# The second alignment's code differences moved from TensorE's fp32 products to VectorE's bf16 operations

## What is computed

```python
D = _pairwise_euclidean(small, large)          # 1601 x 64 per batch
R = _dtw_cost(D)                               # R[i,j] = D[i,j] + min(R[i-1,j], R[i,j-1], R[i-1,j-1])
i_idx, j_idx, valid = _backtrack(R, T_small, T_large)   # choice = argmin([diagonal, up, left])
expanded = zeros.at[j_idx].add(small[i_idx] * valid)
x = x + align(ctx_1024, layernorm(x))          # 32 batches; small = ctx_1024 (1601 rows), large = x (64 rows)
x = x + rwkv(layernorm(x))                     # 4 x 512 tokens, 256 features, 16 heads
x = x + moe(layernorm(x))                      # 8 experts of 704, the best 2 of each token, and a shared one
```

## Time and profile before

| | |
|---|---|
| median of 3 runs | 1171.64 us (1171.23 to 1174.55) |
| span of the profiled execution | 1175.4 us |
| mean granted TensorE clock | 0.938 |
| TensorE busy | 1005.5 us, 86% |
| VectorE busy | 660.5 us, 56% |
| ScalarE busy | 494.2 us, 42% |
| lines 1590 and 1591, both alignments | 68.5 and 63.5 us busy, 144 records each |
| chain that ended last, by engine | TensorE 55%, VectorE 29%, DMA 6%, ScalarE 3% |

### The profile page before, as it was taken

One profiled execution on the slowest core, in us unless ns is written; L12 is line 12 of the kernel. 1 busy time (PEld: TensorE's weight loads), 2 busy tenths in 40 slices (PEclk: granted clock), 3 DMA queues, 4 the chain that ended last, 5 costly groups with the idle time before them and its releaser, 6 DMA issues.

```text
span 1175.4 us, 15523 instructions
## 1 busy us (share of the span) xinstructions
PE 1005.5 (86%) x4892; PEld 598.2 (51%) x4892; DVE 660.5 (56%) x2311; ACT 494.2 (42%) x847; POOL 115.5 (10%) x150
## 2 busy tenths in 40 slices
PE   5886639888891799997899699887999999999998
PEld 2332213333330455553576465645676767676776
DVE  4994949999999776487669612427311111111116
ACT  4885627766781345423242155243222222222221
POOL 1000000000000000000000000000252425242210
PEclk9998979999996799988899799799999999999999
DMA  9999954565876989440050097394121212123115
GB/s 354 324 309 272 274 155 141 154 190 157 237 225 163 327 252 329 135 150 11 1 186 1 0 336 249 104 349 174 49 83 57 83 56 84 56 84 105 32 52 182
DMA packets 123806, 190.47 MB, mean 162 GB/s; under 512 B 9008, under 2 KB 93136, under 8 KB 123728
## 3 DMA queue, kind: packets, MB, share of 16 engines
q1 hardware_dynamic: 117840, 171.13, 47.0%
q0 software_dynamic: 5888, 18.36, 5.1%
HBM read 165.43 MB, written 24.03 MB: 161 GB/s over the span
## 4 chain that ended last, share of the span: by engine, by line
PE 55%; DVE 29%; DMA 6%; issue 4%; ACT 3%; SPq 2%; POOL 0%; DVEq 0%; ACTq 0%; POOLq 0%
PE bank L1816 13%; PE bank L1663 8%; PE bank L1847 7%; PE bank L1684 4%; DVE table L825 4%; PE bank L1808 3%; DMA spaced<-dist 3%; DVE beyond L841 3%; DVE passed L846 3%; PE bank L1827 3%; DVE col_min L818 2%; DVE z L756 2%; PE bank L1590 2%; PE bank L1839 2%; PE bank L1811 2%
## 5 line engine op out<-in xcount | busy, mean ns | idle before, releaser
L1028 DVE TENSOR_TENSOR hid<-bank,act_s 128x352 f32<-128x352 f32 x104 | 54.2, 524 | 220.9 <-PE bank L1816 182.1
L1816 PE MATMUL bank<-w_up,srcT 128*128 x512 | 162.9, 460 | 0.8 <-ACT srcT L1434 0.8
L1574 PE MATMUL bank<-sq,ones 128*64 128x402 f32 (+1 forms) x512 | 101.3, 517 | 38.2 <-ACT sq L1291 38.2
L1442 ACT ACTIVATE act_s<-bank 128x352 f32<-128x352 f32 x104 | 47.9, 463 | 198.4 <-PE bank L1816 127.7
L1816 PEld LDWEIGHTS bank<-w_up,srcT 128*128 128x128 f32 x512 | 96.0, 189 | 47.9 <-issue 4.1
L1590 PE MATMUL bank<-table,ident 128*128 128x402 f32 x144 | 68.5, 560 | 56.3 <-DVE stays L789 51.0
L1568 PE MATMUL bank<-ctxT,latT 128*64 128x402 f32 (+1 forms) x512 | 101.2, 517 | 4.8 <-DMA ctxT<-ctx_tr_dram 4.0
L1663 PE MATMUL bank<-rows_c,on_path 128*64 128x256 f32 (+1 forms) x832 | 100.8, 395 | 2.4 <-DMA rows_c<-ctx_nat_dram 1.6
L1291 ACT ACTIVATE sq<-ctxT 128x1608 f32<-128x1608 f32 x64 | 97.5, 1526 | 8.5 <-DMA ctxT<-ctx_tr_dram 8.5
L1847 PE MATMUL bank<-w_dn,hidT 128*128 (+1 forms) x384 | 93.6, 380 | 0.4 <-DVE y_sb L1042 0.4
L1328 ACT ACTIVATE code<-bank,unpassed 128x402 bf16<-128x402 f32 x72 | 42.1, 589 | 122.9 <-PE bank L1592 122.9
(11 more groups left out here) (292 smaller groups left out, 1619.5 us busy)
## 6 DMA issues: line engine op xcount, KB each, us to landing
rows_c<-ctx_nat_dram SPq DMA_DIRECT2D x32, 896.0 KB
ctxT<-ctx_tr_dram SPq DMA_DIRECT2D x32, 804.0 KB, 8.7
ctxT<-ctx_tr_dram SPq DMA_DIRECT2D x32, 797.0 KB, 7.5
rows_c<-ctx_nat_dram SPq DMA_DIRECT2D x32, 640.0 KB
spaced<-dist SPq DMA_DIRECT2D x128, 101.0 KB, 3.8
w_up<-w_t_dram SPq DMA_DIRECT2D x16, 704.0 KB, 13.3
table<-spaced SPq DMA_DIRECT2D x48, 202.0 KB, 4.2
w_dn<-w_t_dram SPq DMA_DIRECT2D x16, 256.0 KB, 5.8
```

Of the source, the lines that this page charges most:

```text
L1028: e.tensor_tensor(hid[i][:, :], psum[2 * i + 1][:, 0:HH], act_s[i][:, :], ALU.mult).then_inc(hid_done, 1)
L1574: last = e.matmul(ps[b * T:(b + 1) * T, 0:nq], ones[:, 0:T], sq[i][:, b, k, 0:nq], start=False, stop=(k == KC - 1))
L1816: last = e.matmul(psum[2 * i + m][:, 0:HH], srcT[t % 2][:, k, :], w_up[:, bass.ds(ex, 1), m, k, columns], start=(k == 0), stop=(k == KC - 1))
```

## The change

For the second alignment (g = 1) only, TensorE's `code_gap` and ScalarE's `code_bar` are dropped. In their place, for a block q:

- VectorE, step 4q+4, behind `code_stays`: `code_lead`, table row minus `col_min` for the whole block (804 columns), rounded to bf16 in `lead`.
- ScalarE, n = 4q+5: `code_faint`, `stays` times TIE/2 into the one buffer `faint`.
- VectorE, step 4q+6, between the minimum and the scan: `code_lean`, `lead` minus `faint` in bf16. It waits for `code_faint`.
- ScalarE, n = 4q+7: `code_shut`, Relu of `lead` times -PASSED/FAINT into the code, and the edge column.
- VectorE, step 4q+9: `code_final`, now in the second block after instead of the third. It waits for `code_shut`.

The last block is closed on VectorE alone by three dependent operations (`code_last`), and ScalarE only writes its edge. `col_min` and `stays` have two buffers instead of three in the second group, and the memset of the third at its start goes. The first alignment (g = 0) keeps its products, and its waits are the same.

```diff
-MINIMA = [2, 3]
+PLACES = 2
+FAINT = TIE / 2
+def late_faints(n):
+    return [n // CB - 1] if n >= CB and n % CB == 1 else []
+def late_shuts(n):
+    return [n // CB - 1] if n >= CB and n % CB == 3 else []
-        col_min.append(place("col_min2", [CB, L]))
-        stays.append(place("stays2", [CB, LW], BF16))
+        lead, faint = [place(f"lead{i}", [CB, L], BF16) for i in range(2)], place("faint", [CB, L], BF16)
 # VectorE
+            def code_lead(q):
+                tb, k0, n, i = table[1], q * CB, code_width(q), q % 2
+                if q >= 2:
+                    e.wait_ge(shut, q - 1)
+                e.tensor_tensor(lead[i][:, 0:n, :], tb[:, k0 + 1:k0 + n + 1, 0:L], col_min[i][:, 0:n, :],
+                                ALU.subtract).then_inc(led, 1)
+            def code_lean(q):
+                n, i = code_width(q), q % 2
+                e.wait_ge(led, q + 1)
+                e.wait_ge(fainted, q + 1)
+                e.tensor_tensor(lead[i][:, 0:n, :], lead[i][:, 0:n, :], faint[:, 0:n, :],
+                                ALU.subtract).then_inc(leaned, 1)
+            def code_last():
+                q, n = CODES - 1, code_width(CODES - 1)
+                e.wait_ge(stayed, 2 * CODES)
+                e.tensor_scalar(faint[:, 0:n, :], stays[slot_of(q)][:, 0:n, 0:L], FAINT, None, ALU.mult).then_inc(closed, 1)
+                e.wait_ge(led, q + 1)
+                e.wait_ge(closed, 1)
+                rows = lead[q % 2][:, 0:n, :]
+                e.tensor_tensor(rows, rows, faint[:, 0:n, :], ALU.subtract).then_inc(closed, 1)
+                e.wait_ge(closed, 2)
+                e.tensor_scalar(code[1][:, q * CB:q * CB + n, 0:L], rows, -PASSED / FAINT, 0.0, ALU.mult,
+                                ALU.max).then_inc(closed, 1)
             def code_final(g, q):
-                e.wait_ge(barred, half_count(g, q, 1))
+                if g and q == CODES - 1:
+                    e.wait_ge(closed, 3)
+                elif g:
+                    e.wait_ge(shut, q + 1)
+                else:
+                    e.wait_ge(barred, half_count(g, q, 1))
             def align(g):
                     if at == 0 and q >= 1:
                         code_stays(g, q - 1)
+                        if g:
+                            code_lead(q - 1)
                     if at == 1 and q >= places_:
                         code_final(g, q - places_)
+                    if g and at == 2 and q >= 1:
+                        code_lean(q - 1)
 # ScalarE
+            def code_faint(q):
+                n = code_width(q)
+                e.wait_ge(stayed, CODES + q + 1)
+                if q >= 1:
+                    e.wait_ge(leaned, q)
+                e.activation(faint[:, 0:n, :], stays[slot_of(q)][:, 0:n, 0:L], ACT.Copy,
+                             scale=FAINT).then_inc(fainted, 1)
+            def code_shut(q):
+                k0, n = q * CB, code_width(q)
+                e.wait_ge(leaned, q + 1)
+                e.activation(code[1][:, k0:k0 + n, 0:L], lead[q % 2][:, 0:n, :], ACT.Relu,
+                             scale=-PASSED / FAINT).then_inc(shut, 1)
+                code_edge(q)
             def align(g):
                 for n in range(CODE_SLOTS):
-                    for q, h in bar_halves(n):
-                        code_bar(g, q, h)
+                    if g:
+                        for q in late_faints(n):
+                            code_faint(q)
+                        for q in late_shuts(n):
+                            code_shut(q)
+                        if n == STEPS:
+                            code_edge(CODES - 1)
+                    else:
+                        for q, h in bar_halves(n):
+                            code_bar(g, q, h)
 # TensorE
-                    for q, h in code_halves(n):
-                        code_gap(g, q, h)
+                    if g == 0:
+                        for q, h in code_halves(n):
+                            code_gap(g, q, h)
```

35 lines of the change are left out of this document (22 added, 13 removed).

## The result

The changed kernel takes 1180.07 us at the median of 20 runs (1175.0 to 1184.62) against 1175.71 us (1171.23 to 1181.32, 20 runs) for the kernel before: a ratio of 1.0045, 95% interval 1.0032 to 1.0059. It is slower by 4.4 us at the medians and by 5.3 us by the ratio. The forecast was 1167.3 us and a range of 1160 to 1177. The profiled execution of after has a span of 1177.7 us, 2.3 us over that of before, at a mean granted clock of 0.912 (before 0.938). TensorE is busy 959.0 us, 46.5 less; VectorE 683.6 us, 23.1 more; ScalarE 501.9 us, 7.7 more.

A forecast was written before the change was run, and what follows sets the result against it. It took TensorE as busiest in the second alignment's forward scan, with VectorE nearly the bound. Gains and losses summed mark by mark to 4.3 us early, from 1171.64 to 1167.3 us, range 1160 to 1177.

The forecast's parts named there:

- What bounds the kernel: Second alignment's forward scan, 380 to 559 us: TensorE is busiest, but VectorE, busy 107.2 of 162.3 us, is nearly the bound.
- the chain's 41 us: Share of the chain of waits, 22.9% of 179.4 us, on the three removed products; not expected to come back whole.
- rival 2: VectorE absorbs it all: leads and leans cost their full 25 us, gain falls to about 1 us, 1170.6 us; chance 0.12.
- The pieces: VectorE's added work per block: 0.90 us for a lead, 0.38 for a lean, 21.8 us in 17 blocks; `code_last` 1.2.
- The new waits: `code_lean` on VectorE waits for ScalarE's `code_faint`, queued behind masks or gates; 6.2 us at step 10, also steps 42, 46.
- The marks: Running sum at VectorE's marks: 2.7 us late at 404.42, then early by 1.4, 4.2, 6.0, 3.3, 1.8, 2.3 and 4.3.
- two waits of 0.9 us: Before the way back at 559.38: these waits and one `code_final` go, against 1.9 us more for lead and `code_last`.
- 565.22, "these go: 4.3 us early": The `kv` at 565.22 waited 2.04 us for projections behind the last three halves; without that wait, 4.3 us early.
- The trace of before as the base: All mark times of before were taken from its profile, with a profiled execution of 1175.4 us, forecast to become 1171.1.
- Behind 669 nothing changes.: After the second alignment's end at 669 us no further gain or loss, so the 4.3 us stand.
- Rival 3: Slower by the clock: pauses drop TensorE to 1.2 GHz in 455 to 506, 8 us slower, 1179.7 us; chance 0.18.
- Rival 1: TensorE's time comes back more fully: leans don't stall, clock holds near 459 and 540; 11 us gain, 1160.6 us; chance 0.20.

## Why the prediction was wrong, point by point

*What bounds the kernel.* Right that the chain's 41 us wouldn't come back and that VectorE was nearly the bound; even the careful reading still gave the removal too much: the two fp32 products alone are worth 2.6 us. (36 halves of 1.57 us are 56.5 us, not 54, and rival 2's sum is 1171.0 rather than 1170.6; neither bears on the forecast.)

*The pieces.* Nearly exact. A lead pushes the scan by 0.90 us and a lean by 0.38, as forecast (0.90 us from the lead's start at 530.61 to the scan in after's timeline, and 0.77 us from minimum to scan with a lean at 525.84, where a plain step has 0.39). Lead 0.99 us, lean 0.57, `faint` and the last pass 0.87 us each (forecast 0.95); `code_last` is 0.46, 0.48 and 0.47 us behind a lead of 0.78, and takes 1.47 us from its start to the next operation (forecast 1.2). TensorE's records fall by 180, as forecast, but its busy time by 46.5 us and not 60, since more of what is left runs at the lower clock. In the table of traces the stretch from `rms` to the threshold grows with the additions, from 60.2 us (no products) to 64.4 (lead) and 66.9 (lead and lean, mean of six traces of after).

*The new waits.* Right: the leans wait in steps 10, 42, 46 and also in 70, for 5.74, 2.40, 3.25 and 5.23 us. What they cost isn't shown by itself: the later lean took 9.6 us of such waits away (from the kernel with all idle products) and brought 7.2 us of waits for ScalarE's last pass.

*The marks.* Against the one trace of before the forecast said 2.7 late, then 1.4, 4.2, 6.0 early at `rms`, 2.3 early at the threshold. Measured: 2.7 late (407.10), 1.9 (453.19), 6.9 (471.07), 8.1 (490.94), 1.9 early (557.46). So the sum held within 0.4 us up to the way back, by two errors that met: more was gained up to `rms`, and from there to the threshold 6.2 us were lost instead of 3.7. The `kv` of 552.74 still came 3.3 early (549.43; forecast 1.8), so the last miss stands behind it: the sum let two waits of 0.9 us for ScalarE go there, and after waits 1.64 us for ScalarE's last pass instead:

```profile
556.55 0.96 DVE L842 TENSOR_TENSOR code<-stays,code 128x808 bf16<-128x808 bf16 x2 [1.64 <-ACT code L1401]
```

*565.22, "these go: 4.3 us early".* The first failing step. The projection there started cold once more, which no term had:

```profile
557.06 3.78 PE L1769 MATMUL bank<-hT,w_v 128*128 128x512 f32 x4 [4.23 <-ACT gate_r L1480]
```

It takes 3.78 us behind an idle time of 4.23, so `kv` came 2.0 early. And the gain could not have passed in any case: the way back hangs on the threshold, and from there to the end of the terms VectorE needs 107.9 us in before and 107.5 in after. The sum should have ended on the threshold's 2.3, 1169.3 us.

*The trace of before as the base.* The second failing step. The forward part took 287.2 us in the trace from which every mark was counted, and 283.4, 284.8 and 282.2 (283.3 less the 1.1 of delay) in the three others: a mean of 284.4. Six traces of after, the delay taken off, give 285.4. Against the one trace after gains 2.8 us in this part; mean against mean it loses 1.0. By parts: 5.3 gained up to `rms` (116.9 to 111.6), 7.0 lost from there to the threshold (59.9 to 66.9), 0.7 gained on the way back. The lost 7 us are a stretch that VectorE bounds: it is busy 55.59 of 66.6 us there in after, 47.41 of 60.4 in before.

*"Behind 669 nothing changes."* The third failing step and the largest, 4.6 us. The code doesn't change, but TensorE's slow stretches fall on it otherwise: 3.2 of the 4.6 us are lost by the `rms` of the last recurrence, 0.6 of them before `w_r` and `w_w`. The delays show this by themselves: 1.1 us of idle work cost before 3.9, and 1.6 us gave after some 4 back.

With 4.3 cut to 2.3, 2.8 for the base and 4.6 behind 669, the forecast's 4.3 us faster becomes 5.1 us slower; the means of the traces give 1.0 + 4.6 = 5.6, and the ratios 1.0045 and 1.0066 are 5.3 and 7.7 us. The absolute number had a base of its own that was off: the median of 1171.64 us was of 3 runs, that of 20 runs is 1175.71, so 4.1 of the 12.8 us between 1167.3 and 1180.07 come from there. Starts of the second alignment that differ by 0.5 us between the two sets of traces are within their scatter.

*The rivals.* Rival 3 had the size (8 us slower) and the cause, the clock, but not the place: in 455 to 506 the granted clock fell only from 0.93 to 0.90 and 0.8 was never crossed. It fell in 506 to 559 (0.50 and 0.68 against the rows of before in the earlier trace rows) and, without any edit there, in 735 to 775. The rule of the Trainium skill in "TensorE: Matmul & The Clock Gate", section "HAM oscillation — how this bites in real kernels", pointed the same way. This case's traces agree with it in 506 to 530.8, where TensorE is busy 5.55 of 24.80 us at a granted clock of 0.50; behind 669 the clock fell after waits of some 2 us between longer bursts (busy 34.4 of 40 us at 0.74), which isn't the rule's case of bursts shorter than the waits. The mean clock went from 0.938 to 0.912. Rival 1 had no part. Rival 2's prices didn't come (0.90 and 0.38 us held), though the stretch from `rms` to the threshold is bound by VectorE as it says.

What stays open: why, in both traces of a kernel, the slow stretches stand in nearly the same place to the work (71.3 and 71.6 us behind the end of the terms in after, 72.6 and 72.5 in before), though that end itself moves by 2 to 4 us against the start of the span (664.96 and 667.01, 667.24 and 663.58). Nor is it shown why the two sets of idle products don't add, or what costs the 1.4 us behind the last gate.

A version that beats both kernels came out of it: after with the four idle products behind 669, 0.9959 of before (0.994 to 0.9978), 3 to 5 us. With three of the four it was 0.9999 on another chip, so the margin is small.

## What to carry to other kernels

Where an edit takes work off a TensorE that is also the pacing engine, price each pause that it opens, and ask what a shift of one or two microseconds does to all the TensorE work downstream: here that was larger than the edit. A filler works only where it meets the fall of the clock: the same four products gave after 7.4 us and before nothing. Take the base of a blind sum from several traces, or give its scatter (here 282.2 to 287.2 us) as a bound, and let the sum end on the mark that the next stretch hangs on, not on the last one that moved. A share in the chain of waits is not a prize: take the work away without its substitute first, and see what is left to win.

## What the runs showed of the hardware

A kernel can become faster by 4 us through 1.6 us of idle work on VectorE, and slower by 3.9 through 1.1 us, and the rows that differ most are TensorE's `w_r` and `w_w`, at the lower clock in one case (3.62 and 2.77 us) and not in the other (1.88 each). Three idle fp32 products of 512 columns, some 3 us of TensorE time (1.02 us each), gave 7.0 us back. And a bf16 subtraction or scaling of 603 columns takes VectorE 0.46 to 0.48 us, of 804 columns 0.57: 201 columns more cost some 0.1 us.
